# A graph network in one launch: the last stage's bias products become adds on VectorE and ScalarE, and seventeen blocks of layer 2 stay in SBUF in place of eight

## The reference, cut to what matters

```python
# layer 0
edge_feat = gelu((x[src] + edge_attr) @ W_pre + b_pre, approximate=False) * bases
y = x + segment_sum(edge_feat, dst, 50000)
h = relu(bn(y @ W1 + b1, g1, be1))          # bn: mean and variance over the nodes
h = relu(bn(h @ W2 + b2, g2, be2))
x = layernorm(x + y + h)
# layer 1
S = x[src]
def edge_nn(x, W, b):
    h = relu(x @ W.T + b)
    return relu(h @ W.T + b)                # the same W and b twice
msgs = where(rel == r, edge_nn(S, W_rel[r], b_rel[r]))     # two relations
agg = segment_sum(msgs, dst, 50000)
i, f, g, o = split(agg @ W_ih.T + b_ih + b_hh, 4)
c = sigmoid(i) * tanh(g)
hn = sigmoid(o) * tanh(c)
x = layernorm(x + (relu(relu(hn @ W1.T + b1) @ W2.T + b2) @ W3.T + b3))
```

## Time and profile before

| | |
|---|---|
| runs | 2007.58, 2014.62, 2010.78 us, median 2010.78 |
| profiled execution | 2016.65 us, its span 2014.9 us |
| mean granted clock of TensorE | 0.962 |
| busy, share of the span | TensorE 89%, its weight loads 69%, VectorE 79%, ScalarE 64%, GpSimd 53% |
| moved | 516.22 MB, mean 256 GB/s |
| `edges0` and layer 1 | 0 to some 630 us |
| layer 2 | some 635 to 935 us |
| `dense3` | some 937 to 1358 us |
| `edges1` | 1360 us to the end |

### The profile page before, as it was taken

How to read it: one execution, slowest core, us unless ns; L and a number is a source line. 1 busy time by engine, 2 the same in 40 slices (tenths; PEclk the granted TensorE clock), 3 DMA queues, 4 the chain that set the end, 5 groups by cost and what they waited for, 6 DMA issues and landing times. The chain is left out here.

```text
span 2014.9 us, 27432 instructions
## 1 busy us (share of the span) xinstructions
PE 1791.8 (89%) x8697; PEld 1398.7 (69%) x8697; DVE 1601.0 (79%) x2326; ACT 1295.1 (64%) x1818; POOL 1075.1 (53%) x1200
## 2 busy tenths in 40 slices
PE   4677589999998999999999999956999999999994
PEld 3465478888886776766666666635888888888883
DVE  4688456766767999997999999994888888888883
ACT  1434246566656898886888888862566666666663
POOL 7556446776785400001555555557776566654443
PEclk8899789999999999999999999987999999999997
DMA  9999999999995899994999999965654423222210
GB/s 343 368 352 393 363 357 339 337 342 330 342 236 135 244 350 343 333 344 157 351 388 384 389 412 392 385 247 137 174 157 138 118 89 92 92 83 79 65 41 29
DMA packets 190577, 516.22 MB, mean 256 GB/s; under 512 B 26757, under 2 KB 80111, under 8 KB 190178
## 3 DMA queue, kind: packets, MB, share of 16 engines
q1 hardware_dynamic: 132898, 389.66, 52.7%
q0 software_dynamic: 47136, 73.62, 16.2%
q10 hardware_dynamic: 10400, 51.20, 6.6%
HBM read 328.87 MB, written 241.07 MB: 283 GB/s over the span
## 5 line engine op out<-in xcount | busy, mean ns | idle before, releaser
L618 POOL DMA_INDIRECT scratch_y<-sums,k_target x196 | 313.4, 1599 | 156.1 <-issue 70.2
L1040 ACT ACTIVATE d_o<-d_u,d_free 128x256 f32<-128x256 f32 x392 | 203.1, 589 | 64.6 <-POOL d_free L1077 64.4
L1014 PEld LDWEIGHTS d_pN<-k_ident,d_r 128*128 128x128 f32 x1568 | 192.1, 193 | 52.1 <-issue 46.4
L1009 PE MATMUL d_pN<-d_y,d_free 128*128 128x512 f32 x392 | 192.0, 612 | 33.3 <-DVE d_u L1103 29.3
L821 ACT ACTIVATE d_part_h<-pT 128x1024 fp32r<-128x1024 f32 x98 | 100.5, 1026 | 150.7 <-PE pT L788 137.0
L1014 PE MATMUL d_pN<-k_ident,d_r 128*128 128x128 f32 x1568 | 192.7, 277 | 4.9 <-ACT d_r L1029 4.9
L882 DVE TENSOR_TENSOR d_part_l<-pT,d_part_h 128x1024 fp32r<-128x1024 f32 x98 | 119.9, 1225 | 85.8 <-ACT d_part_h L821 85.8
L1074 POOL TENSOR_TENSOR d_free<-d_free,k_minus_half 128x8 f32<-128x8 f32 (+1 forms) x100 | 163.6, 1636 | 0.2
L1103 DVE SCALAR_TENSOR_TENSOR d_u<-d_pN,d_free,k_base 128x256 f32<-128x256 f32 x392 | 161.0, 474 | 0.0
L256 POOL DMA_INDIRECT k_ring<-in_x,k_src x100 | 123.6, 1236 | 66.5 <-PE pT L284 37.8
L60 PE MATMUL pU<-d_part_h,k_w_h 128*128 128x512 f32 x296 | 125.9, 425 | 26.7 <-DVE d_part_l L882 13.7
(11 more groups left out here) (232 smaller groups left out, 5192.6 us busy)
## 6 DMA issues: line engine op xcount, KB each, us to landing
scratch_h<-d_h SPq DMA_DIRECT2D x168, 512.0 KB, 5.7
out<-d_o SPq DMA_DIRECT2D x97, 520.0 KB, 5.9
k_ring<-scratch_y SPq DMA_DIRECT2D x98, 512.0 KB, 7.8
d_y<-scratch_y SPq DMA_DIRECT2D x98, 512.0 KB, 7.7
scratch_y<-in_x ACTq DMA_DIRECT2D x25, 2000.0 KB, 20.2
d_h<-scratch_h SPq DMA_DIRECT2D x90, 512.0 KB, 7.0
k_ring<-scratch_h SPq DMA_DIRECT2D x78, 512.0 KB, 5.3
attr<-in_attr_t SPq DMA_DIRECT2D x25, 512.0 KB, 15.2
```

The lines of the kernel that those rows point to most:

```text
L618: pool.indirect_dma_start(out=A["y"], out_offset=bass.IndirectOffsetOnAxis(ap=K.target[:, t:t + 1], axis=0), in_=K.sums[:, t], in_offset=N ...
L1009: pe.matmul(pN[k % 4][:, 2 * two:2 * two + 2].rearrange("p j f -> p (j f)"), twice[:], y[:, k % 4, two * 2 * F:(two + 1) * 2 * F], start=T ...
L1014: last = pe.matmul(pN[k % 4][:, j, cc * P:(cc + 1) * P], r[:, k % 4, cc, j * P:(j + 1) * P], K.ident[:], start=False, stop=j % 2 == 1 and ...
L1040: last = act.activation(o[:, k % 4, j, 0:F], u[:, k % 3, j], ACT.Identity, bias=nb[:, n, j:j + 1], scale=rs[:, n, J + j:J + j + 1])
```

## The change: what it does

In the last stage, the two bias products, the row tile and the float32 flags are gone. VectorE adds the difference of the two biases where the edge has relation 1 (`add_bias`, from PSUM to SBUF), and ScalarE's relu adds the bias of relation 0, now from SBUF and in place. `mlp3` waits for `biased`, VectorE's read of the bank. VectorE's adds stand at the end of an iteration, behind the low part of hn. SP no longer loads `has_k`, and so has no wait for `m_done`. In the first stage `message_biases` (four instructions) stands in place of `bias_rows` (twelve), on products with four columns in place of 256. `KEPT` is 17: four blocks in `held`, four in the ring of h2 blocks, three in the place of the raw weights, two in a free part, four in the ring `h` of stage 2, for which ScalarE now waits until the stores from its slots have landed. ScalarE's wait for all of the scatters comes nine passes sooner, as does the end of the stores.

```diff
-HELD, KEPT = 4, 8
+HELD, KEPT = 4, 17
+KEPT_WEIGHTS, KEPT_FREE, FREE_USED = 3, 2, 512
...
         # edges0, SP
-        sp.dma_start(rows, A["rows"]).then_inc(wm_full, 16)
...
-                sp.dma_start(A["has"].rearrange("r (t p) -> t r p", p=P), has_f[:]).then_inc(has_kept, 16)
...
         # edges0, TensorE, last small product
-                    for ic in range(C):
-                        last = pe.matmul(pS[0:4, r], b4[:, ic], raw_rel[:, r, ic], start=ic == 0, stop=ic == C - 1)
+                    for oc in range(C):
+                        for ic in range(C):
+                            at = r * C + oc
+                            last = pe.matmul(pS[:, 0, at * 4:(at + 1) * 4], raw_rel[:, r, ic, oc * P:(oc + 1) * P],
+                                             b4[:, ic], start=ic == 0, stop=ic == C - 1)
...
-        def bias_rows():
-            ...
+        def message_biases():
+            through = pS[:, 0, 0:2 * C * 4].rearrange("p (r c o) -> p r c o", r=2, o=4)
             dve.tensor_tensor(out=K.shift[:], in0=b3[:], in1=K.base[:], op=ALU.subtract)
+            dve.tensor_tensor(out=second_bias[:], in0=through[:, 1, :, 1], in1=K.rel_b[:, C:2 * C], op=ALU.add)
+            then(dve.tensor_tensor(out=K.msg_b[:], in0=through[:, 0, :, 0], in1=K.rel_b[:, 0:C], op=ALU.add))
+            dve.tensor_tensor(out=K.msg_db[:], in0=second_bias[:], in1=K.msg_b[:], op=ALU.subtract).then_inc(side_ready, 1)
...
         # dense12
+        def kept_at(n):
+            raw_wl, free = K.shared_sums[5].rearrange("p b o -> p (b o)"), K.shared_sums[6][:, FREE_USED:]
+            for space, size in ((held, HELD), (K.shared_sums[0], 4), (raw_wl, KEPT_WEIGHTS), (free, KEPT_FREE)):
+                if n < size:
+                    return space[:, n] if len(space.shape) == 3 else space[:, n * C * B:(n + 1) * C * B]
+                n -= size
+            return h[:, (len(stores) + n) % 4]
...
+            ringed = g - (2 * NB - 4)
+            if ringed >= 0:
+                act.wait_ge(stored[(len(stores) + ringed) % 4], 16 * ((len(stores) + ringed) // 4))
             if g == 2 * NB - KEPT + HELD:
                 for q in range(4):
                     act.wait_ge(halved_in[q], 16 * ((ET - 1 - q) // 4 + 1))
...
         # dense3
-            block_k = second.held[:, k] if k < HELD else h2[:, k % 4]
+            block_k = second.kept_at(k) if k < KEPT else h2[:, k % 4]
...
         # edges1, SP
-                if k >= 0 and k + 2 < EB:
-                    load_has_k(k + 2)
-                    if k + 3 < EB:
-                        load_has(k + 3)
+                if k >= 0 and k + 3 < EB:
+                    load_has(k + 3)
...
         # edges1, TensorE, second_layer and mlp3
-                pe.wait_ge(has_k_full[k % 2], 32 * (k // 2 + 1))
-                    pe.matmul(pL[:, oc, wide(k)], K.rows[:, oc * P:(oc + 1) * P], has_k[:, k % 2, wide(k)], start=True, stop=False)
...
-                pe.wait_ge(msg_done, C * min(k + 2, EB))
+                pe.wait_ge(biased, C * min(k + 2, EB))
...
         # edges1, ScalarE, message
-                    act.wait_ge(m_done, C * k + cc + 1)
-                    if k >= 2:
-                        act.wait_ge(agg_lo, C * (k - 2) + cc + 1)
-                        act.wait_ge(summed, C * (k - 1) + cc + 1)
-                    act.activation(msg[:, k % 2, cc, wide(k)], pL[:, cc, wide(k)], ACT.Relu).then_inc(msg_done, 1)
+                    act.wait_ge(biased, C * k + cc + 1)
+                    act.activation(msg[:, k % 2, cc, wide(k)], msg[:, k % 2, cc, wide(k)], ACT.Relu,
+                                   bias=K.msg_b[:, cc:cc + 1]).then_inc(msg_done, 1)
...
         # edges1, VectorE
+            def add_bias(k, cc):
+                dve.wait_ge(m_done, C * k + cc + 1)
+                if k >= 2:
+                    dve.wait_ge(agg_lo, C * (k - 2) + cc + 1)
+                    dve.wait_ge(summed, C * (k - 1) + cc + 1)
+                dve.scalar_tensor_tensor(out=msg[:, k % 2, cc, wide(k)], in0=has[:, k % 4, 1, wide(k)], scalar=K.msg_db[:, cc:cc + 1],
+                                         in1=pL[:, cc, wide(k)], op0=ALU.mult, op1=ALU.add).then_inc(biased, 1)
...
-            dve.memset(has_k[:].bitcast(F32), 0.0).then_inc(has_k_clear, 1)
...
                     low(hnp, hn, k, hn_hi, hn_lo, k + 1)
+                if real(k + 1):
+                    add_bias(k + 1, 0)
+                    add_bias(k + 1, 1)
```

More of the change, by code:

```diff
@@ L147, in edges0 @@
     raw_m = spare[:, 1024:1024 + (NBLK - M1) * P].rearrange("p (n o) -> p n o", o=P)
[L148 to L151, removed]
+    second_bias = sb("second_bias", [P, C])
     has_u8 = small[0:S.TC, 2 * P:2 * P + P // 2].bitcast(U8).rearrange("p (r e) -> p r e", r=2)
@@ L244, in _ @@
         sp.wait_ge(need_kept, 64)
-        sp.wait_ge(has_kept, 32)
+        sp.wait_ge(has_kept, 16)
     @block.gpsimd
@@ L312, in base_mlp @@
             if n == 0:
-                pe.wait_ge(wm_full, 64)
+                pe.wait_ge(wm_full, 48)
                 for ic in range(C):
@@ L510, in _ @@
         for r in range(2):
-            dve.tensor_scalar(out=has_u8[:, r], in0=rel_i[:], scalar1=float(r), scalar2=None, op0=ALU.is_equal)
-            dve.tensor_scalar(out=has_f[:, r], in0=rel_i[:], scalar1=float(r), scalar2=None,
+            dve.tensor_scalar(out=has_u8[:, r], in0=rel_i[:], scalar1=float(r), scalar2=None,
                               op0=ALU.is_equal).then_inc(has_done, 1)
@@ L643 @@
     stores: int
-    held: object
+    kept_at: object
     kept: list
@@ L927, in _ @@
         coef2_vector(dve)
-    return SecondStage(stored, halved_in, h_done, coef2_ready, coef2_pool, len(stores), held, [k for _, k in passes[2 * NB - KEPT:]])
+    return SecondStage(stored, halved_in, h_done, coef2_ready, coef2_pool, len(stores), kept_at, [k for _, k in passes[2 * NB - KEPT:]])
 def dense3(nc, A, K, S, c, used, block, second):
@@ L950, in dense3 @@
     pN = K.pN
+    assert 320 + 2 * 4 * J <= FREE_USED
     h2_full, y_full, o_out = ([sem(f"d3_{name}{n}") for n in range(4)] for name in ("h2_full", "y_full", "o_out"))
@@ L1162, in edges1 @@
         pY = pM[:].rearrange("p (j f) -> p j f", j=J)
-        xd_full, has_k_full = ([sem(f"{n}{b}") for b in range(2)] for n in ("xd_full", "has_k_full"))
+        xd_full = [sem(f"xd_full{b}") for b in range(2)]
         xs_first, xs_full = ([sem(f"{n}{b}") for b in range(4)] for n in ("xs_first", "xs_full"))
@@ L1205, in _ @@
         def _(sp):
-            def load_has_k(k):
-                if k >= 2:
[L1208 to L1211, removed]
             def load_has(k):
@@ L1371, in second_layer @@
                             last = mm3(pe, pL[:, oc, wide(k)], (K.wl_h[:, blk], K.wl_l[:, blk]),
-                                       (hidp[r][0][:, ic, wide(k)], hidp[r][1][:, ic, wide(k)]), False,
+                                       (hidp[r][0][:, ic, wide(k)], hidp[r][1][:, ic, wide(k)]), r == 0 and ic == 0,
                                        r == 1 and ic == C - 1)
@@ L1638, in __init__ @@
         self.w0_h, self.w0_l = sb("w0_h", [P, 3, C, F], F32R), sb("w0_l", [P, 3, C, F], F32R)
-        self.rows, self.shift = sb("rows", [P, F], F32R), sb("shift", [P, F])
+        self.shift = sb("shift", [P, F])
+        self.msg_b, self.msg_db = sb("msg_b", [P, C]), sb("msg_db", [P, C])
         self.src, self.dst_gather = sb("src", [P, S.TC], I32), sb("dst_gather", [P, S.TC], I32)
@@ L1666, in build @@
     A["cont"] = nc.dram_tensor("scratch_cont", (S.TC * P,), U8, kind="Internal").ap()
-    A["has"] = nc.dram_tensor("scratch_has", (2, S.TC * P), F32, kind="Internal").ap()
     A["has_u8"] = nc.dram_tensor("scratch_has_u8", (2, S.TC * P), U8, kind="Internal").ap()
@@ L1766, in laid_out @@
         "wt": np.stack(wt, 1), "cols": np.concatenate(cols, 1),
-        "rows": np.concatenate([i["L1_gnn_b_rel"]] * 2, 0),
         "rel_r": edges_to(i["edge_type_2"], 0).reshape(S.TC, P),
```

12 lines of the change are left out of this document (3 added, 9 removed).

## The result

The changed kernel takes 2006.67 us in the median of 12 runs (2002.94 to 2010.67), the kernel before, run beside it, 2014.99 us (12 runs, 2007.58 to 2019.99). The ratio is 0.996, 95% interval 0.9949 to 0.997: 8.3 us less, against the 8.0 forecast. The two spans therefore differ by 13.6 us, of which some 5 are scatter; I read stages and periods, not spans.

What follows compares the result with a forecast made beforehand. The prediction took TensorE to bound the last stage, at 24.45 us a block. It summed 7.5 us saved there and 0.5 in the first stage to 8.0, from 2010.78 to 2002.8 us, range 1999 to 2006.

Steps and rivals of the forecast that it cites:

- Part 1: Last stage, two bias products removed: 0.467 us less a block, 24.45 to 23.98 us, a ceiling of 10.3 us in all.
- Part 2: Last stage, VectorE's two adds: scan 0.22 us later, saving cut to 7.4 us over 22 periods.
- the row of `hidden`: Last stage, recorded time of the nearest VectorE instruction, 0.746 us, taken as the price of one add.
- Two kinds of blocks: Last stage: 13 quick periods saving 0.45 us each, 9 others at 24.28 us saving 0.17 each.
- the place of the new wait: Last stage, the other blocks: TensorE waits for VectorE's low part of m1 before the second MLP product.
- the slack of the other blocks: Last stage, loop through VectorE and ScalarE: about 0.39 us of slack in 8 of 20 blocks, 0.73 in quick ones.
- rival A: Last stage: the loop of VectorE and ScalarE sets every block, some 2.5 us saved, 2008.3 us; chance 0.22.
- TensorE still sets it: Last stage, quick blocks: the loop needs 23.94 us, below TensorE's 23.98, so TensorE keeps the pace; 0.45 us saved each.
- The ends: Ends of the last stage: 0.4 us saved in block 0, 0.3 us lost where the blocks become narrow.
- Part 3: Last stage's queues: the byte-wide load and the clearing of its tile go, nothing on the path waits for them; 0.
- Part 4: First stage: four VectorE instructions for twelve, 4.1 us becoming 1.0; 0.5 us saved, bounds 0 and 3.3.
- Part 5: Layer 2 and dense stage: nine blocks less stored and loaded, transfers hidden; 0.

Runs made afterwards that it cites:

- e3: The kernel before without its two bias products a block in the last stage, message bias left out; ratio to before 0.9921.
- e5: The changed kernel with two unused tiles that put the last stage's tiles back at their old addresses; ratio to the kernel before 0.9988.
- e6: The changed kernel with the scaling of the source rows moved from VectorE to ScalarE; 2000.14 us, ratio to the kernel before 0.9922.
- e8: The changed kernel again, unedited, on the chip of a later group; ratio to the kernel before 0.9967.
- e7: The changed kernel with TensorE's wait for VectorE's low part moved from the second MLP's first product to its third; ratio to the kernel before 0.9955.
- e11: The kernel before with an unused 64-byte tile that moves the last stage's tiles from 160 to 224 bytes modulo 256; ratio to before 0.9964.
- e1: The kernel before with only the block keeping changed: seventeen blocks of layer 2 stay in SBUF in place of eight; ratio to before 1.0008.
- m2: TensorE alone, chains of 60 products, two places of the weights against sixteen of the moving operand; 0.227 to 0.234 us a product.
- e9: The changed kernel with two unused tiles putting weights of the first stage and layers 1 and 2 at 224 bytes modulo 256; 2004.06 us, ratio to before 0.9937.

## Why the prediction was right, and where not

**Part 1** holds as worked out: e3 shows 23.97 us for 23.98.

**Part 2**, its first half holds: the adds take 0.70 us each (0.75 where one stands alone), the relu 0.72 us, the scan starts 0.23 us later (0.22). Of the two prices for the add, the row of `hidden` was the right one; the estimate of 0.66 us from the Trainium skill, "VectorE: DVE Perf Modes", section on the TRN2 errata, is below the 0.75 recorded. Two kinds of blocks and the place of the new wait came true in e5, with 11 quick and 10 others for the forecast's 13 and 9. Two terms were mis-sized. The first is the slack of the other blocks, an error of arithmetic: of the 12.8 us of idle time in 20 blocks the 12 quick ones have 12 x 0.73 = 8.8, which leaves 0.50 us for each of the 8, not 0.39. With it their period is 24.17 us; e5 shows 24.12 to 24.17. What makes them slow is the scaling of the rows, 0.24 us longer there, which rival A named among the causes that it left open. The second is TensorE's pace in the changed kernel, which wasn't 0.233 us a product: the row tile and the tile of flags left SBUF, the tiles behind them moved by 5056 bytes, from 160 to 224 modulo 256, onto the place of the weights. With that TensorE's own period is some 23.5 us (e6), and **the step that failed is "TensorE still sets it" in quick blocks**: the loop of VectorE and ScalarE sets every block, at 23.86 and 24.10 us. That is rival A's mechanism without its price, since A took the slow blocks' length for all. Both lengths are 0.07 to 0.08 us below what the waits gave (23.94 and 24.17); no run shows why.

The two parts of the gain can be told apart by the periods, here without the one that was 28.2 us in e5. The other 21 take 513.3 us before, 505.6 in e5 and 502.6 in the changed kernel: 7.7 us by the change proper (forecast 7.4 for 22), 3.0 us by the addresses (e5 ran in another group than the changed kernel; e8, in a third, has 502.6 us too). All 22 periods are 11.2 us shorter than before, and 9.9 in e8; the medians show 8.3, 2 us uncertain, and in e8 6.1, 3 us uncertain. That 8.0 was met so closely is therefore in part luck: the sum lacked the 3 us of the addresses, and about as much was lost, or is scatter, outside these periods; no run shows which.

**The ends.** The scatter hides them. The first two periods of the stage are together 38.81 us before, 38.54 in the changed kernel, 38.39 in e8 and 38.93 in e7; the forecast had 0.4 us less. In block 0 the first scan waits for the second add too, the queue being in order.

**Part 3**: nothing on the path waits for SP in the stage after, as said.

**Part 4**: four instructions of 0.1 to 0.4 us took the place of the twelve, and VectorE is as full as before (19.86 of 20 us). In the profiles of the first comparison and of e6, e7, e8 and e11 the dense stage starts between 928.8 and 934.7 us, in the two of the unedited changed kernel 2.7 us apart: 0.5 us can't be told from that. No run tried this part alone.

**Part 5**: 0, as the steps of e1 and of the changed kernel show.

## What to carry to other kernels

Work that is moved from the engine that sets the pace to one that has the smallest slack in the loop pays only until that loop takes over. Read the next bound from the waits that end on the pace of the bounding engine, and add them up for each kind of block by itself. Before a change to tile sizes is credited with a gain, put the other tiles back at their old addresses, since adding or dropping a small tile can move the matmuls' operands against their weights, which was worth 3 us here beside the edit's 8, and in e11 as much as the whole change. A wait of the busiest engine doesn't name the bound: e7 moved that wait away and the time stayed, e6 relieved the loop behind it and the time fell.

## What the runs showed of the hardware

TensorE's 512-column fp32r products at 2.4 GHz (granted clock 1.00) step 0.227 us when weights and moving operand start at the same place modulo 256 bytes of SBUF, 0.229 with the moving operand 64 bytes past, 0.232 to 0.234 otherwise (m2). The same shows in the last stage (0.233 in e5, 0.227 to 0.229 in e11) and in layer 1 (0.228 in e9, 0.233 in e11). The Trainium skill, "TensorE: Matmul & The Clock Gate", section "Step-by-step: what each phase is for", says that the array has two independent SBUF read ports, so that loading weights doesn't take read bandwidth from the running product. By that the distance of the two operands should not matter; m2 has it matter by 3% of the step, so they do not seem wholly independent, though no run shows where they would meet. The same page, section "Back-to-back issue gap", has 216 ns as the gap of a single product of 512 columns, without naming a type; the fp32r products of m2, each with its weight load, did not step below 227.
